# In the last feed-forward of batch 0, ScalarE copies the up projection to SBUF and GpSimd forms the gated product; loops written out

## The reference

```
topk_scores, topk_indices = jax.lax.top_k(scores, 32)        # L1_xattn, 16 heads
...
x = x + _L1_xattn_ref(...)
...
g = jnp.einsum('td,efd->etf', xt, Wg)                        # L1_ffn
u = jnp.einsum('td,efd->etf', xt, Wu)
h = jax.nn.relu(g) * u
out_e = jnp.einsum('etf,edf->etd', h, Wd)
out = jnp.einsum('te,etd->td', combine, out_e)
```

## Time and profile before

| what | value |
|---|---|
| median of the runs | 704.72 us (3 runs, 702.49 to 706.40) |
| span of the profiled execution | 699.2 us (its own time is not listed beside it) |
| TensorE busy | 601.7 us, 86% |
| VectorE busy | 448.5 us, 64% |
| ScalarE busy | 292.0 us, 42% |
| GpSimd busy | 224.3 us, 32% |
| chain that ended last | PE 60%, DVE 28%, ACT 5%, issue 4%, POOL 2% |
| instruction fetch | queue 8: 24 packets, 0.39 MB; queue 14: 24 packets, 0.20 MB |

### The profile page before, as it was taken

The page is one execution under the profiler, slowest core; times in us unless marked ns, Lnnn a source line. Parts: engine busy times, 40 slices in busy tenths (PEclk is TensorE's granted clock), DMA queues, the critical chain, the costliest instruction groups (busy, mean ns, idle before and its releaser), DMA issues.

```text
span 699.2 us, 13228 instructions
## 1 busy us (share of the span) xinstructions
PE 601.7 (86%) x4091; PEld 468.9 (67%) x4091; DVE 448.5 (64%) x2353; ACT 292.0 (42%) x685; POOL 224.3 (32%) x202
## 2 busy tenths in 40 slices
PE   5874479977999999888999997858999998789997
PEld 3654269963665666645666666747888877678886
DVE  3655777524435344469898999688999995343333
ACT  2321123313665656255555554224445544234542
POOL 3001500001343433325454455333445543122220
PEclk9955579996999999999999998868999999999999
DMA  5000003300000000000030000101111111113120
GB/s 163 25 0 0 1 0 93 90 23 0 13 24 11 13 22 12 11 1 13 13 102 0 1 2 1 46 0 46 46 46 46 45 46 46 45 46 91 47 59 15
DMA packets 35629, 22.86 MB, mean 33 GB/s; under 512 B 2224, under 2 KB 32380, under 8 KB 35581
## 3 DMA queue, kind: packets, MB, share of 16 engines
q1 hardware_dynamic: 35581, 22.27, 10.9%
HBM read 21.74 MB, written 0.52 MB: 32 GB/s over the span
## 4 chain that ended last, share of the span: by engine, by line
PE 60%; DVE 28%; ACT 5%; issue 4%; POOL 2%; DMA 0%; DVEq 0%; ACTq 0%; POOLq 0%
PE ps L1482 49%; DVE wk L973 8%; DVE top L964 5%; PE ps L1795 4%; DVE cat_mem L1092 2%; PE ps L1985 2%; DVE nmax L928 2%; PE ps L1837 2%; DVE hits L827 1%; PE ps L1494 1%; ACT w_mem L1312 1%; PE ps L1712 1%; DVE bn L658 1%; DVE xn L671 1%; PE ps L1755 1%
## 5 line engine op out<-in xcount | busy, mean ns | idle before, releaser
L928 DVE TENSOR_REDUCE nmax<-ps 128x2 f32<-128x256 f32 (+1 forms) x64 | 52.6, 822 | 66.2 <-PE ps L1482 65.7
L1482 PE MATMUL ps<-cat_mem 128*128 128x128 f32 (+1 forms) x528 | 77.6, 291 | 10.1 <-DVE cat_mem L1092 10.1
L1092 DVE TENSOR_TENSOR cat_mem<-gr,ps 128x512 f32<-128x512 f32 x64 | 43.7, 684 | 58.7 <-ACT gr L1425 58.1
L973 DVE MATCH_REPLACE8 wk<-top,wk 128x77 f32<-128x77 f32 x384 | 80.5, 224 | 0.0
L1482 PEld LDWEIGHTS ps<-cat_mem 128*128 128x128 f32 x528 | 67.3, 196 | 16.8 <-DVE cat_mem L1092 13.7
L552 POOL TENSOR_TENSOR w_mem<-w_mem,rinv 128x768 f32<-128x768 f32 (+1 forms) x32 | 53.7, 1679 | 54.1 <-DVE rinv L934 54.1
L1324 ACT ACTIVATE cat_mem<-ps 128x512 f32<-128x512 f32 x48 | 28.6, 596 | 93.8 <-PE ps L1985 93.8
L609 POOL TENSOR_TENSOR w_lo<-cat_mem,w_hi 128x512 fp32r<-128x512 f32 x32 | 41.1, 1286 | 70.6 <-ACT w_hi L1327 70.4
L1482 PE MATMUL ps<-x_hi,w_hi 128*128 128x512 f32 x128 | 58.7, 458 | 2.9 <-ACT x_hi L1412 2.9
L964 DVE MAX8 top<-wk 128x8 f32<-128x77 f32 x384 | 58.0, 224 | 0.0
L497 POOL TENSOR_TENSOR rstd<-var_eps,minus_half 128x4 f32<-128x4 f32 x12 | 12.3, 1022 | 135.5 <-DVE var_eps L664 135.3
(11 more groups left out here) (257 smaller groups left out, 1270.8 us busy)
## 6 DMA issues: line engine op xcount, KB each, us to landing
w_mem<-in_L_ffn_W_dram SPq DMA_DIRECT2D x16, 256.0 KB, 3.0
cat_mem<-in_L_ffn_Wg_dram SPq DMA_DIRECT2D x16, 256.0 KB, 2.9
cat_mem<-in_L_ffn_Wu_dram SPq DMA_DIRECT2D x16, 256.0 KB, 3.3
cat_mem<-in_L_ffn_Wd_dram SPq DMA_DIRECT2D x16, 256.0 KB, 3.8
wn<-in_L_attn_w_q_dram SPq DMA_DIRECT2D x16, 64.0 KB, 1.7
wn<-in_L_attn_w_k_dram SPq DMA_DIRECT2D x16, 64.0 KB, 1.9
wn<-in_L_attn_w_v_dram SPq DMA_DIRECT2D x16, 64.0 KB, 1.9
x<-in_x_dram SPq DMA_DIRECT2D x2, 256.0 KB, 3.1
```

The lines of the kernel that those rows point to most:

```text
L928: dve.tensor_reduce(nmax[:, c, :], ps[:, 2 * s:2 * s + 2, 0:n], X, ALU.max, negate=True)\
L973: dve.match_replace(wk[q][:, t, h, :], top[q][:, t, h, 8 * r:8 * r + 8], src[:, t, h, :], GONE).then_inc(top_step, 1)
L1092: dve.tensor_tensor(hg[s][:, :], gr[s][:, :], ps[:, 2 * s + 1, :], ALU.mult)\
L1482: return pe.matmul(dst, lhsT, rhs, start=start, stop=stop, skip_group_check=shared)
```

## The change

In batch 0 of the last feed-forward (j < 32) the gate product moves from VectorE to GpSimd. GpSimd is given its up projection in SBUF: ScalarE copies it behind the Relu into `us`, which lies in the two buffers `prT` that the attention has finished with. `up(j)` now waits for copy j - 2 (`up_ready`), as this frees the banks; `relu(j)` waits for product j - 2, as this frees `gr` and `us`. On GpSimd the products stand between gone/pick, shift, and the two halves of w_lo. In batch 1 VectorE forms the products as before. All `Fori` loops, on all engines, become Python loops, that is straight code with constants in place of registers.

```diff
+        us = [prT[s][:, 0, :] for s in range(2)]
...
-            def weights_lo(m, q):
-                for k in range(2):
+            def weights_lo(m, q, kinds=(0, 1)):
+                for k in kinds:
...
+            def gate(j):
+                s = j % 2
+                pool.wait_ge(gr_ready, j + 1)
+                pool.wait_ge(up_ready, j + 1)
+                pool.tensor_tensor(hg[s][:, :], gr[s][:, :], us[s][:, :], ALU.mult).then_inc(hg_ready, 1)
...
-            with pool.Fori(0, NP // 2 - 1) as i:
-                for q in range(2):
-                    n = NP + 2 * i + q
-                    gone(n, q)
-                    pick(n, q)
-                    shift(n + 1, 1 - q)
-                    weights_lo(2 * i + q + 1, 1 - q)
+            for m in range(E - 2):
+                q = m % 2
+                gone(NP + m, q)
+                pick(NP + m, q)
+                gate(FC * m)
+                shift(NP + m + 1, 1 - q)
+                gate(FC * m + 1)
+                weights_lo(m + 1, 1 - q, (0,))
+                gate(FC * m + 2)
+                weights_lo(m + 1, 1 - q, (1,))
+                gate(FC * m + 3)
             gone(2 * NP - 2, 0)
             pick(2 * NP - 2, 0)
+            gate(FC * (E - 2))
             shift(2 * NP - 1, 1)
-            weights_lo(E - 1, 1)
+            gate(FC * (E - 2) + 1)
+            weights_lo(E - 1, 1, (0,))
+            gate(FC * (E - 2) + 2)
+            weights_lo(E - 1, 1, (1,))
+            gate(FC * (E - 2) + 3)
             gone(2 * NP - 1, 1)
             pick(2 * NP - 1, 1)
-            weights_lo(E, 0)
+            gate(FC * (E - 1))
+            gate(FC * (E - 1) + 1)
+            weights_lo(E, 0, (0,))
+            gate(FC * (E - 1) + 2)
+            weights_lo(E, 0, (1,))
+            gate(FC * (E - 1) + 3)
             rstd_of(11)
             tokens_lo(1)
...
                 for jj in range(FC):
-                    gate(FC * m + jj, jj % 2)
+                    if m >= E:
+                        gate(FC * m + jj, jj % 2)
...
             def relu(j, s):
                 act.wait_ge(gu_ps, j + 1)
+                if 2 <= j < FC * E:
+                    act.wait_ge(hg_ready, j - 1)
                 act.activation(gr[s][:, :], ps[:, 2 * s, :], ACT.Relu).then_inc(gr_ready, 1)
+                if j < FC * E:
+                    act.activation(us[s][:, :], ps[:, 2 * s + 1, :], ACT.Copy).then_inc(up_ready, 1)
...
-                if later(j, 2):
+                if j >= FC * E + 2:
                     pe.wait_ge(hg_ready, j - 1)
+                elif j >= 2:
+                    pe.wait_ge(up_ready, j - 1)
...
-            with pe.Fori(0, NP // 2 - 1) as i:
+            for i in range(0, NP // 2 - 1):
```

More of the change, by code:

```diff
@@ L152, in decoder @@
         gr_ready = semaphore("gr_ready")
+        up_ready = semaphore("up_ready")
         d_ps = semaphore("d_ps")
@@ L452, in _ @@
                 load_a1(q, q)
-            with sp.Fori(0, E // 2 - 1) as i:
+            for i in range(0, E // 2 - 1):
                 for q in range(2):
@@ L457, in _ @@
             for b in range(B):
-                with sp.Fori(0, NP // 2 - 1) as i:
+                for i in range(0, NP // 2 - 1):
                     for q in range(2):
@@ L587, in pair @@
                 divide(TB * g + 3, 3)
-            with pool.Fori(0, NP) as g:
+            for g in range(0, NP):
                 for c in range(TB):
@@ L598, in _ @@
             pair(NP + 1, 0, 0)
-            with pool.Fori(0, 2) as i:
+            for i in range(0, 2):
                 for k in range(2):
@@ L627, in _ @@
             add_bo(1)
-            with pool.Fori(0, NP // 2 - 1) as i:
-                for q in range(2):
-                    n = NP + 2 * i + q
-                    gone(n, q)
-                    pick(n, q)
-                    shift(n + 1, 1 - q)
-                    weights_lo(2 * i + q + 1, 1 - q)
+            for m in range(E - 2):
[9 more added lines that the diff above has]
+                gate(FC * m + 3)
             gone(2 * NP - 2, 0)
             pick(2 * NP - 2, 0)
+            gate(FC * (E - 2))
             shift(2 * NP - 1, 1)
-            weights_lo(E - 1, 1)
+            gate(FC * (E - 2) + 1)
[3 more added lines that the diff above has]
+            gate(FC * (E - 2) + 3)
             gone(2 * NP - 1, 1)
             pick(2 * NP - 1, 1)
-            weights_lo(E, 0)
+            gate(FC * (E - 1))
[4 more added lines that the diff above has]
+            gate(FC * (E - 1) + 3)
             rstd_of(11)
             tokens_lo(1)
-            with pool.Fori(E // 2, E - 1) as i:
+            for i in range(E // 2, E - 1):
                 for q in range(2):
@@ L909, in _ @@
                 expert0(q, q)
-            with dve.Fori(1, E // 2 - 1) as i:
+            for i in range(1, E // 2 - 1):
                 for q in range(2):
@@ L1128, in _ @@
             pair(0, 0)
-            with dve.Fori(0, NP // 2 - 1) as i:
+            for i in range(0, NP // 2 - 1):
                 for k in range(2):
@@ L1135, in _ @@
             pair(NP + 1, 1, k=0)
-            with dve.Fori(0, 2) as i:
+            for i in range(0, 2):
                 for k in range(2):
@@ L1163, in _ @@
                     add_context(1, 4)
-                gate(FC * (E - 1) + jj, jj % 2)
                 if jj == 0:
@@ L1174, in _ @@
             expert1(E + 1, 1, 1)
-            with dve.Fori(E // 2 + 1, E - 1) as i:
+            for i in range(E // 2 + 1, E - 1):
                 for q in range(2):
@@ L1288, in _ @@
                 expert0(q, q)
-            with act.Fori(1, E // 2 - 1) as i:
+            for i in range(1, E // 2 - 1):
                 for q in range(2):
@@ L1379, in _ @@
             pair(0, 0)
-            with act.Fori(0, NP // 2 - 1) as i:
+            for i in range(0, NP // 2 - 1):
                 for k in range(2):
@@ L1391, in _ @@
             pair(NP + 1, 1, k=0)
-            with act.Fori(0, 2) as i:
+            for i in range(0, 2):
                 for k in range(2):
@@ L1471, in _ @@
             expert1(E + 1, 1)
-            with act.Fori(E // 2 + 1, E - 1) as i:
+            for i in range(E // 2 + 1, E - 1):
                 for q in range(2):
@@ L1741, in _ @@
                 expert0(q, q)
-            with pe.Fori(1, E // 2 - 1) as i:
+            for i in range(1, E // 2 - 1):
                 for q in range(2):
@@ L1965, in _ @@
             pair(NP + 1, 1, 1, k=0)
-            with pe.Fori(0, 2) as i:
+            for i in range(0, 2):
                 for k in range(2):
@@ L2103, in _ @@
             expert1(E + 1, 1, 1)
-            with pe.Fori(E // 2 + 1, E - 1) as i:
+            for i in range(E // 2 + 1, E - 1):
                 for q in range(2):
```

## The result

The changed kernel takes **708.46 us** (median of 20 runs, 704.17 to 713.26), the kernel before 702.46 us (20 runs, 700.11 to 707.13): ratio **1.0073**, 95% interval 1.0053 to 1.0094. The time lies in the forecast range and 1 us from its 707.5, but much of that is luck: the three runs that were shown before had a median of 704.72, 2.3 us above that of twenty. By difference I had said +2.8 us (+0.40%). It is +6.0 us between the medians (0.85%), and about +5.1 us by the ratio, which is estimated from all the runs (0.73%). By my bound of 0.5% the likeliest case was "no change", and "slower" came. The profiled span went from 699.2 to 706.8 us, +7.6.

A forecast was written before the change was run, and what follows sets the result against it. VectorE was taken to bound the stage, with TensorE's floor close behind. +0.5 + 2.0 + 1.7 + 0.4 - 1.8 = +2.8 us on the 699.2 span gives 702.0; with 5.5 for the median, 707.5, range 700.5 to 711.5.

The forecast's parts named there:

- my bound of 0.5%: Whole kernel: a measurement tells about 0.5%, 3.5 us, from no change; chances faster 0.22, within 0.43, slower 0.35.
- Entry to expert 1: Expert 0 into expert 1, batch 0: first down projection waits for GpSimd's late product, +2.0 us, then low clock, +1.7.
- the contention and the queue: Entry to expert 1: GpSimd slows `gates` by 1.9 us, product stands behind gone and pick; `down(1,0)` 2.0 us later.
- the low clock: Entry to expert 1: TensorE idles 4.2 us, then a window at half clock; +1.7 us (bounds 0 and 5).
- Steady experts, +0.5: Five experts of batch 0: about 15.3 us each against 15.2, TensorE trading one wait for two; +0.5 us.
- the two waits: Each steady expert: TensorE waits for GpSimd, 0.42 us before `down(m,1)` and 0.43 us before `up(m+1,0)`.
- End of the stage, +0.4: Last expert and norm, batch 0: GpSimd's last product delays rstd from 602.49 to 602.9; +0.4 us.
- The loops, -1.8: Loops written out: 1.0 us in batch 0's attention, 0.9 with the top-32 beside it; -1.8 us (bounds 0 and -2.8).
- The top-32 pairs: Attention with the top-32 beside it: 0.45 us left at most per pair, four pairs, half taken: 0.9 us.
- (1): Batch 0's experts: products arrive in time, both waits go, no low clock or contention; -4.7 us, 700.0; chance 0.20.
- (2): In `gates`: no contention, all else as forecast, +0.2 us in place of +2.0; 705.7; chance 0.20.
- (3): Batch 0's experts: low clock in each second one, 5.1 us, or products of 1.45 us; up to 712.6; chance 0.20.

The follow-up runs named there:

- the quiet kernel: The changed kernel with gate products 2 and 3 of expert 0 on VectorE, from ScalarE's copies; 707.16 us, ratio to before 1.0051.
- gate(4) first: The changed kernel with GpSimd forming the first product of expert 1 ahead of gone and pick, in that expert alone; 703.68 us, ratio to before 1.0001.
- the moved take-over: The changed kernel with experts 0 and 1 as in the kernel before, GpSimd taking the products from expert 2 on; 709.53 us, ratio to before 1.0076.
- the copies alone: The changed kernel with all products back on VectorE, which reads ScalarE's copy in SBUF; 706.63 us, ratio to before 1.0042.
- all loops kept: The changed kernel with its hardware loops not written out, products on GpSimd and copies on ScalarE; 713.42 us (6 runs), ratio to before 1.0150.
- the loops alone: The kernel before with every hardware loop written out and nothing else changed; 702.58 us against 702.15, ratio 1.0001.
- products first everywhere: The changed kernel with the first product ahead of gone and pick in every expert from 1 on; 711.50 us (6 runs), ratio to before 1.0129.

## Why the prediction was right and where it was wrong

**Entry to expert 1: mechanism right, size close.** I had +2.0 for the contention and the queue and +1.7 for the low clock, 3.7 together; the trace has 4.02 + 0.31. Counted from the tokens of batch 0, `down(1,0)` came 2.7 us later than before (2.0 forecast), and the remaining 1.7 us go with the low clock. `up(1,1)` came at 489.50, which counted so is the 488.7 of the forecast. The contention was sized at 1.9: `rred`, `comb` and `comb` took 0.47, 1.22 and 1.28 us in the chain, where the quiet kernel has 0.19 for each `comb`, so 2.1 for those two alone. TensorE's idle time was 3.53 and 0.92 us, I had 4.2. The low clock came, 3.4 us at 0.50. That the late product makes this loss is shown by gate(4) first (1.0001) and by the moved take-over (19.15 us in expert 2). What I had not seen is why it is the entry and only the entry: I put the late `gone` on `gates`, and without `gates` it is as late, since VectorE is the late engine up to there.

The Trainium skill's page "SBUF — State Buffer", section "SBUF: two separate sides", says that VectorE and GpSimd share a pair of ports that one of them holds for a whole instruction, if VectorE's has two SBUF inputs. By that rule, the runs agree: 1.22 and 1.28 against 0.19 us, and 1.77 against 0.68.

**Steady experts, +0.5: the picture held, the sum had the wrong base.** The period is 15.34 to 15.38 us (15.3 forecast), with the two waits where I put them, and the five take 76.50, 0.5 above five times 15.2. But before's five had taken 77.01 us with their stretch of low clock, which stands in the span that I added to. After has no low clock there; so the difference is -0.51.

**End of the stage, +0.4: mechanism right.** Measured +0.68, with 3.4 us of low clock in either trace. TensorE's wait for the last product went from 1.57 to 2.18 us, and VectorE's for rstd, which stands behind that product (until 606.8) in GpSimd's queue, from 0.56 to 2.23.

**The loops, -1.8: the step that failed.** The pairs of the attention of batch 0 were read rightly, 12.67 to 12.53 us for six pairs. The top-32 pairs, for which I had taken 0.9 (1.0 + 0.9 is 1.9, not the 1.8 of the sum), gained nothing: 18.28 us at full clock in both, so the shorter straight pair of 17.29, which moreover had a low stretch in it (clock 0.90), told of its smaller work and not of the loop. The feed-forward's loops, for which I had taken nothing, gave 0.9 in five experts. And the whole moves the time by nothing (1.0001, -1.7 to +1.9 us): low clock ahead of the feed-forward and in the last expert outweighs it. That the loops cause these stretches isn't shown. In company of GpSimd's products the loops seem to matter: 1.0150 with them and 1.0073 without, about 5 us, from six runs against twenty. The traces place 0.7 to 0.8 of these in experts 2 to 6, and the rest is open.

**What the sum left out, +2.2:** the feed-forward of batch 1, in which nothing was changed. Its first 20 us have clock 0.74 against 0.91 in the windows above: 10.2 us at the lower level in place of 3.4. I had rivals for a low clock that comes back beside the experts, none behind them. Every kernel with ScalarE's copies, the copies alone among them, lost 1.5 to 3.1 us there but one (all loops kept, 95.3, whose low clock of 10.2 us came in the last expert), and gate(4) first lost 1.5 too and came out even. In before TensorE stood 1.57, 0.56 and 1.35 us around the norm ahead of this stage, and in after 2.18, 1.03 and 1.35. These longer waits are a candidate for the cause, but the kernel with all loops kept has the same three and no low clock behind them. So the cause stays open, and with it 2.2 of the 7.6 us.

**The rivals.** (1) fell as posed, but its core can be had: with both waits of an expert gone it takes 14.71 us, and then the clock takes more than that back: experts 2 to 6 took 79.0 and 78.4 us in the two kernels that have it, 76.5 after. (2), no contention, fell: it was there. (3), the low clock in each second expert, did not come with the two waits in place; it came when the waits were taken away.

None of the twelve kernels beats the kernel before. Gate(4) first and the loops alone equal it within 0.3%.

## What to carry to other kernels

Work moved from a late engine to one that waits for it was queued behind that lateness once, in the round in which it was handed over, at both places tried here: look there at what stands ahead of it in the new engine's order, and at the steady state separately, since the order that suits one hurts the other. Before counting the relief of an engine that is 97% busy, read how busy the second one is, and whether the clock is still granted at the rate that the second one would reach. And a gain in one stage counts only once the next stage has started earlier: compare the starts, stage by stage.

## What was unexpected about the hardware

In the middle of the stage TensorE's granted clock went down where the engine had the least idle time: where an expert takes 14.71 us at full clock, with one wait of 0.32 us in it, four of five had a stretch of 1.2 GHz, and three of them took up to 16.35 us. With the waits for the product and for w_lo in place, 0.28 us idle at the first and 0.66 us more for the expert (15.37), the clock stayed at 1.00 for five experts. It isn't the whole rule: the copies alone had one low stretch in experts of 15.47 us, and products first everywhere had two behind experts of 15.65. Over the runs of one kernel a spread of 7 us goes with the clock: the changed kernel took 704.2 and 704.6 us in its runs of clock 0.921 and 710.9 to 712.0 in those of 0.902.
